# A chunked state-space stage: decay prefixes from one scan per batch, x weighted on ScalarE, scores made four chunks at a time

## The reference

```python
zxbca = x @ W_in.T
x_t, z_t, b_t, c_t, a_log = split(zxbca)      # 32 heads, 64 wide
decay = exp(-exp(a_log))                       # one number per token and head
def step(states, inp):
    xt, bt, ct, dec = inp
    states = states * dec[:, :, None, None] + xt[..., None] * bt[:, :, None, :]
    yt = einsum('bhpn,bhn->bhp', states, ct) + xt * D
    return states, yt
y = scan(step, ...); y = y * silu(z_t); y = layernorm(y) * gamma + beta
return y @ W_out.T
```

## Time and profile before

| | us |
|---|---|
| median of 3 runs (lowest, highest) | 2042.74 (2037.55, 2045.25) |
| the profiled execution | 2042.33 |
| its span | 2040.3 |
| busy: PE / PEld / DVE / ACT / POOL | 1826.9 / 1623.2 / 1412.7 / 781.5 / 734.3 |
| mean granted TensorE clock | 0.965 of 2.4 GHz |
| chain that ended last, by engine | PE 63%, DVE 15%, POOL 8%, issue 8%, ACT 6% |

### The profile page before, as it was taken

How to read it: one execution, slowest core, us unless ns; L and a number is a source line. 1 busy time by engine, 2 the same in 40 slices (tenths; PEclk the granted TensorE clock), 3 DMA queues, 4 the chain that set the end, 5 groups by cost and what they waited for, 6 DMA issues and landing times.

```text
span 2040.3 us, 33554 instructions
## 1 busy us (share of the span) xinstructions
PE 1826.9 (90%) x11376; PEld 1623.2 (80%) x11376; DVE 1412.7 (69%) x3170; ACT 781.5 (38%) x1846; POOL 734.3 (36%) x772
## 2 busy tenths in 40 slices
PE   5998999999898888988969989999998988888889
PEld 4996777888787777877849967778887877788878
DVE  5555887545688888887455558875456888888874
ACT  3334454332333333334632344543323333333355
POOL 1012443001566666662010124430014666666610
PEclk9999999999999999998969999999998999999989
DMA  2120000021112211210021200000211122121100
GB/s 77 45 100 16 16 17 23 11 73 47 49 58 66 66 60 59 66 55 1 16 70 45 100 16 17 16 23 10 73 45 48 61 65 65 66 65 60 50 6 16
DMA packets 39446, 93.75 MB, mean 46 GB/s; under 512 B 3632, under 2 KB 12464, under 8 KB 38768
## 3 DMA queue, kind: packets, MB, share of 16 engines
q1 hardware_dynamic: 39280, 91.62, 13.4%
HBM read 89.24 MB, written 2.36 MB: 45 GB/s over the span
## 4 chain that ended last, share of the span: by engine, by line
PE 63%; DVE 15%; POOL 8%; issue 8%; ACT 6%; DMA 0%; DVEq 0%; SPq 0%; POOLq 0%; ACTq 0%
PE ps L495 27%; PE ps L567 11%; PE ps L536 5%; DVE pdec L1513 4%; PE ps L789 3%; PE ps L559 3%; POOL w_in_lo L477 3%; PE ps L781 2%; POOL y L472 2%; PE ps L771 2%; PE ps L523 2%; PE ps L669 2%; ACT cTz L1119 2%; POOL rb L420 2%; PE ps L650 2%
## 5 line engine op out<-in xcount | busy, mean ns | idle before, releaser
L472 POOL TENSOR_TENSOR y<-yg,sz 128x128 f32<-128x128 f32 x256 | 220.4, 861 | 324.7 <-DVE yg L1561 324.7
L1131 ACT ACTIVATE xz_x<-ps 128x128 f32<-128x128 f32 x256 | 71.2, 278 | 426.3 <-PE ps L495 366.2
L567 PE MATMUL ps<-w_out,yT 128*128 128x256 f32 x1024 | 226.0, 379 | 0.0
L567 PEld LDWEIGHTS ps<-w_out,yT 128*128 128x128 f32 x1024 | 192.3, 190 | 24.9
L420 POOL TENSOR_TENSOR rb<-ra,rb 128x512 f32<-128x512 f32 x80 | 118.6, 1483 | 221.8 <-DVE rb L1372 221.7
L468 POOL TENSOR_TENSOR xd<-xz_x,d_row 128x128 f32<-128x128 f32 x256 | 176.6, 690 | 47.2 <-ACT sz L1134 47.2
L781 PEld LDWEIGHTS ps<-xw,b_tok 128*128 128x128 f32 x448 | 79.9, 189 | 115.4 <-issue 106.6
L781 PE MATMUL ps<-xw,b_tok 128*128 128x128 f32 x448 | 91.0, 285 | 83.5 <-DVE ssm_state L1549 46.9
L1513 DVE TENSOR_TENSOR_SCAN pdec<-dec,dstart 64x512 f32<-64x512 f32 x128 | 161.6, 1263 | 0.9
L789 PE MATMUL ps<-xz_x,mt 128*128 128x128 f32 x1024 | 160.3, 280 | 1.6 <-DVE yg L1561 1.6
L1529 DVE TENSOR_TENSOR xw<-ps,lmat 128x128 f32<-128x128 f32 x256 | 72.9, 285 | 124.6 <-ACT sz L1134 124.6
(11 more groups left out here) (172 smaller groups left out, 4993.6 us busy)
## 6 DMA issues: line engine op xcount, KB each, us to landing
dec<-dec_dram SPq DMA_DIRECT2D x64, 512.0 KB, 3.9
w_raw<-in_w_in SPq DMA_DIRECT2D x32, 512.0 KB, 3.6
w_raw<-in_gu SPq DMA_DIRECT2D x14, 704.0 KB, 4.1
w_raw<-in_w_qkv SPq DMA_DIRECT2D x8, 768.0 KB, 4.5
dn_raw<-in_dn SPq DMA_DIRECT2D x14, 384.0 KB, 4.7
w_out<-in_w_o SPq DMA_DIRECT2D x2, 2048.0 KB, 11.3
w_out<-in_w_out SPq DMA_DIRECT2D x2, 2048.0 KB, 8.5
x_res<-in_x SPq DMA_DIRECT2D x8, 256.0 KB, 3.6
```

Source lines behind the costliest of these rows:

```text
L472: nc.gpsimd.tensor_tensor(y[:, c, bass.ds((2 * i + w) * P, P)], yg[:, s], sz[:, s], ALU.mult).then_inc(s_out.sem, 1)
L567: mm = nc.tensor.matmul(ps[:, 4 + s, 0:DM], yT[:, s, t, :], w_out[:, t, :], start=(t == 0), stop=(t == NT - 1))
```

## The change

- **Decay prefixes.** `pdec` is no longer scanned per unit. Once per batch, in the last FFN group, DVE scans all 32 heads at a time (`decay_prefix`: 32 partitions x 1024 tokens, in five steps), SP writes the decays (with chunk starts zeroed) and the prefixes to DRAM, and loads the prefixes per unit as two broadcasts of 64 partitions into `pdec`. `dstart`, its copies and the memset in `dec` are gone.
- **Weighted x.** `xw` is made by ACT, two copies of 128 x 64 from PSUM with the column of `lmat` as per-partition scale, between `xz_x` and `sz`.
- **Scores.** `unit_scores` makes the four score matmuls of a unit in one run, in the third chunk of the unit before, and DVE weights them two chunks at a time (two products of 512 columns). The matmul itself, one of 256 columns for both heads against the zero-padded `cTz`, is the same as before.
- **Order.** `b_turn` moves to the head of the fourth chunk, ACT's `c_copy` and `btok_copy` move ahead of `xz_copy`. The increments of `settled` go. The first weight load of the stage comes behind the writes of the prefixes, and the two `lmat` scans of the first unit move from chunks 3 and 4 of the last FFN group to 5 and 6.

```diff
@@ sync @@
-                sp.wait_ge(s_dec.sem, s_dec.done(b))
-                sp.dma_start(dec_dram, dec_t[:]).then_inc(dec_out, 16)
-                sp.wait_ge(dec_out, 16 * (b + 1))
...
-                        weights(split_ssm(b, h), a["w_in"][bass.ds(h, 1)].rearrange("g p c -> p (g c)"), KT * XZBC)
...
-                            sp.wait_ge(s_scan.sem, s_scan.done(2 * n + hf - 2))
-                            sp.dma_start(dec[:, :, toks], dec_dram[bass.ds(2 * h, 2), toks].partition_broadcast(P)).then_inc(dec_in[hf], 16)
+                sp.wait_ge(s_prep, 5 * (b + 1))
+                sp.dma_start(dec_dram[0], dec_t[:]).then_inc(dec_out, 16)
+                sp.dma_start(dec_dram[1], dec_p[:]).then_inc(dec_out, 16)
+                sp.wait_ge(dec_out, 32 * (b + 1))
+                for h in range(HP):
+                    n = b * HP + h
+                    weights(split_ssm(b, h), a["w_in"][h], KT * XZBC)
+                    sp.wait_ge(s_out.sem, s_out.done((n - 2) * NC + NC - 1))
+                    sp.dma_start(d_row[:, h % 2, :], a["d_skip"][h:h + 1, :].broadcast_to([P, P])).then_inc(d_in[h % 2], 16)
+                    for hf in range(2):
+                        u = 2 * n + hf
+                        toks = slice(hf * HALF, (hf + 1) * HALF)
+                        sp.wait_ge(s_scan.sem, s_scan.done(2 * (u - 2) + 1))
+                        sp.dma_start(dec[:, :, toks], dec_dram[0, 2 * h:2 * h + 2, toks].partition_broadcast(P)).then_inc(dec_in[hf], 16)
+                        sp.wait_ge(s_st.sem, s_st.done(4 * (u - 2) + 3))
+                        for k in range(2):
+                            sp.dma_start(pdec[64 * k:64 * k + 64, toks],
+                                         dec_dram[1, 2 * h + k:2 * h + k + 1, toks].broadcast_to([64, HALF])).then_inc(pdec_in[hf], 16)
@@ tensor @@
+                    for j in range(4):
+                        c, m = 4 * hf + j, 4 * u + j
+                        if ahead and j == 3:
+                            b_turn(u + 1, nhf)
+                        if ahead or j < 3:
+                            project_xz(m + 1, nw if j == 3 else n % 2, (c + 1) % NC)
+                        if ahead and j == 2:
+                            unit_scores(u + 1, nhf)
+                        ssm_update(u, m, c)
+                        ssm_outputs(u, m, c)
+                        if ahead and j == 0:
+                            if hf == 1:
+                                ssm_weights(n + 1)
+                            project_b(u + 1, nw, nhf)
+                        if ahead and j == 1:
+                            project_c(u + 1, nw, nhf)
@@ scalar @@
                 def first_pair():
-                    act.wait_ge(dec_out, 16 * (b + 1))
+                    act.wait_ge(dec_out, 32 * (b + 1))
                     ssm_prep(0, 0)
...
-                                         ps[:, 2 + s, 0:P].rearrange("p (h c) -> p h c", c=64), ACT.Copy)
+                                         ps[:, 2 + s, 0:P].rearrange("p (h c) -> p h c", c=64), ACT.Copy).then_inc(s_xcopy.sem, 1)
+                    for h in range(2):
+                        if c % 4 == 0:
+                            act.wait_ge(s_scan.sem, s_scan.done(2 * u + h))
+                        ins = nc.scalar.activation(xw[:, s, 64 * h:64 * h + 64], ps[:, 2 + s, 64 * h:64 * h + 64], ACT.Copy,
+                                                   scale=lmat[:, h, (c + 1) * P - 1:(c + 1) * P])
+                    ins.then_inc(s_xw.sem, 1)
                     act.wait_ge(s_out.sem, s_out.free(m, 2))
...
+                        if ahead and j == 2:
+                            c_copy(u + 1, 1 - hf)
+                        if ahead and j == 3:
+                            btok_copy(u + 1, 1 - hf)
+                        if ahead or j < 3:
+                            xz_copy(u + (j == 3), m + 1, (c + 1) % NC)
+                        if ahead and j == 1:
+                            b_copy(u + 1, 1 - hf)
+                        if hf == 0 and j == 0 and n + 1 < HP:
+                            ssm_prep(n + 1, (n + 1) % 2)
@@ vector @@
+                    nc.vector.memset(dec_s[:], 0.0).then_inc(s_prep, 1)
...
+                    for hf in range(2):
+                        toks = slice(hf * HALF, (hf + 1) * HALF)
+                        nc.vector.tensor_tensor_scan(dec_p[:, toks], dec_t[:, toks], dec_s[:, toks], 0.0, ALU.mult, ALU.add).then_inc(s_prep, 1)
...
+                        ssm_next_state(m, c)
+                        add_skip(m, c)
...
+                        if j < 2:
+                            decay_scan(u + 1, j)
+                        if j == 2:
+                            c_decayed(u + 1)
+                            decayed_scores(u + 1, 0)
+                        if j == 3:
+                            decayed_scores(u + 1, 1)
+                u0 = 2 * b * HP
+                ffn_group(b, G0 + 1, 1, False, {0: decay_prefix, 5: lambda: decay_scan(u0, 0), 6: lambda: decay_scan(u0, 1)}, last=True)
```

More of the change, by code:

```diff
@@ L784, in ssm_outputs @@
                     out = ps[:, 6, 0:P]
-                    pe.wait_ge(s_mt.sem, s_mt.done(m))
                     pe.wait_ge(s_xcopy.sem, s_xcopy.done(m))
                     pe.wait_ge(s_yg.sem, s_yg.done(m - 1))
+                    if c % 2 == 0:
+                        pe.wait_ge(s_mt.sem, s_mt.done(2 * u + c % 4 // 2))
                     for h in range(2):
-                        nc.tensor.matmul(out, mt1[:, c % 2, h * P:(h + 1) * P], xz_x[:, c % 2, h * P:(h + 1) * P],
+                        nc.tensor.matmul(out, mt1[:, u % 2, c % 4, h, :], xz_x[:, c % 2, h * P:(h + 1) * P],
@@ new lines, in ssm_unit @@
+                def ssm_unit(u):
+                    hf = u % 2
+                    n, ahead = u // 2 - b * HP, u < 2 * HP * (b + 1) - 1
+                    nw, nhf = (n + hf) % 2, 1 - hf
+                    for j in range(4):
+                        c, m = 4 * hf + j, 4 * u + j
[13 more added lines that the diff above has]
+                            project_c(u + 1, nw, nhf)
@@ new lines, in xz_copy, with ssm_unit @@
+                    ins.then_inc(s_xw.sem, 1)
+                    act.wait_ge(s_out.sem, s_out.free(m, 2))
+                    nc.scalar.activation(sz[:, s, :], ps[:, 2 + s, P:2 * P], ACT.Silu).then_inc(s_sz.sem, 1)
+                def ssm_unit(u):
+                    hf = u % 2
+                    n, ahead = u // 2 - b * HP, u < 2 * HP * (b + 1) - 1
+                    for j in range(4):
+                        c, m = 4 * hf + j, 4 * u + j
+                        if ahead and j == 2:
[8 more added lines that the diff above has]
+                            ssm_prep(n + 1, (n + 1) % 2)
@@ L1154, in _ @@
                 c_copy(u, 0)
[L1155 removed]
+                xz_copy(u, u * 4, 0)
                 btok_copy(u, 0)
                 gate_silu(b, GRP - 1)
[L1158 to L1160 removed]
+                for u in range(2 * b * HP, 2 * (b + 1) * HP):
+                    ssm_unit(u)
                 end_phase(act, b, 5)
@@ new lines, in decay_scan @@
+                def decay_scan(u, h):
+                    hf = u % 2
+                    toks = slice(hf * HALF, (hf + 1) * HALF)
+                    if h == 0:
+                        dve.wait_ge(dec_in[hf], 16 * (u // 2 + 1))
+                        dve.wait_ge(s_mt.sem, s_mt.done(2 * (u - 2) + 1))
+                        dve.wait_ge(s_xw.sem, s_xw.done(4 * u - 5))
+                    nc.vector.tensor_tensor_scan(lmat[:, h, toks], dec[:, h, toks], ident4[:, 0:HALF], 0.0, ALU.mult, ALU.add).then_inc(s_scan.sem, 1)
@@ L1601, in _, with ssm_unit @@
-                for i in range(0, HP // 2 - 1):
-                    ssm_pairs(i, False)
-                ssm_pairs(HP // 2 - 1, True)
+                def ssm_unit(u):
+                    hf = u % 2
+                    n, ahead = u // 2 - b * HP, u < 2 * HP * (b + 1) - 1
+                    for j in range(4):
+                        c, m = 4 * hf + j, 4 * u + j
+                        ssm_next_state(m, c)
+                        add_skip(m, c)
+                        if n == HP - 1 and c < 2 * EARLY:
+                            dve.wait_ge(s_out.sem, s_out.done((b * HP + 4 * EARLY) * NC - 1))
+                            dve.wait_ge(o_yn.sem, o_yn.done(4 * (b * 2 + 1) * NC - 1))
+                            inner_stats(c // EARLY, c // EARLY, c % EARLY)
+                        if not ahead:
+                            continue
+                        if j < 2:
[5 more added lines that the diff above has]
+                            decayed_scores(u + 1, 1)
```

231 lines of the change are left out of this document (56 added, 175 removed).

## The result

The changed kernel takes **2057.54 us** (median of 4 runs, 2054.37 to 2064.2), the kernel before, run beside it, 2040.35 (2037.55 to 2045.25): ratio **1.0086**, interval 1.0052 to 1.0120. So it is slower by 0.9%, a small step but clear of the interval; the forecast was 2016, range 1985 to 2050, with 0.16 for slower. The profiled execution took 2064.2, its span is 2062.4 and its mean granted clock 0.955 (before 0.965).

A forecast was written before the change was run, and what follows sets the result against it. The prediction took the SSM stages as bound by PE plus one DVE burst per unit. From 2042.3 us it took 35 for 32 pairs at 25.05 instead of 26.17, added 10 for the stage starts: 2017, put at 2016; range 1985 to 2050.

The forecast's parts named there:

- new wait 2: Next pair's w_raw load, queued behind pdec loads on SP, lands late and delays ACT and the scores: 0.65 us a pair.
- the weights land late: Rival, 12%: w_raw lands slower beside other loads; from a landing of 4.4 no gain is left, at 4.7 2051 us.
- the clock falls after each stop: Rival, 7%: the new waits, 2 us together, cause a low-clock stretch in every pair: +38 us, 2054.
- The waits before the increment: PE's waits for DVE's state before line 781, 1.37 and 1.48 us a pair, claimed to go.
- POOL's piece: Last quarter of the weights' low part, awaited by PE before project_b of chunk 4: 0.2 us a pair (0.51 before).
- PE's bare work: PE's work in a pair without its lost time, taken as 22.8 us.
- Wait 1: Scores one project_xz behind project_c wait for ACT's copies of c: 0.7 us a unit, 1.4 a pair.
- the start of the stage: In the last FFN group, prefix writes delay the first w_raw, so ACT and PE stand: +5 us a batch, +10 in all.
- the 6.2: Upper bound for the prefix write to DRAM at the stage's start, 6.2 us against 3 taken: +6 us in all.
- The weights are no wait: Rival, 16%: ACT reaches the split late anyway, or the load lands in under 3 us: 1992 us.
- The lost time only moves: Rival, 10%: POOL's late pieces cost 0.9 us more per pair at chunk 4: +29, about 2043 us, no change.
- DVE's burst: The two pdec scans, 2.54 us per unit on DVE, held to delay the state PE wants; claimed to go.

The follow-up runs named there:

- experiment 2: Changed kernel, next pair's weight load ahead of the two pdec loads but still behind SP's wait for the state; 1990.65 us, ratio 0.9721.
- experiment 6: Kernel before, with SP made to wait for the last chunk's state before loading the next pair's weights; 2064.57 us, ratio 1.0074.
- experiment 1: Changed kernel, next pair's weight load issued ahead of SP's wait for the state and the pdec loads; 1983.68 us, ratio 0.9686.
- experiment 3: Kernel of experiment 1, with the next unit's scores moved behind update and outputs of the third chunk; 1929.02 us, ratio 0.9417.
- experiment 8: Kernel of experiment 3 with the stage's first weights loaded early, unsplit by write waits, plus POOL's four weight pieces behind chunks 0, 1, 2, 2; 1901.58 us, ratio 0.9275.
- experiment 10: Kernel of experiment 3 with the stage's first weights early, plus two unused 64 x 512 scans per unit put back on DVE; 1952.87 us, ratio 0.9522.
- experiment 7: Kernel of experiment 3 with the stage's first weights early, and xw moved back from ACT to DVE; 1929.31 us, ratio 0.9419.
- experiment 11: Changed kernel, next pair's weight load moved further back on SP, behind d_row and the first half's dec; 2172.69 us, ratio 1.0604.

## Why the prediction was wrong

**The step that failed is new wait 2.** "Two `pdec` issues at some 0.4 each; `w_raw` at 0.85; it lands 3.6 later, at 4.45." It was issued at 1.28 and used 4.4 later in the middle, at 5.6 (in the pair shown 4.86 later, at 6.14). Both parts come from the `pdec` loads beside it in the queue. They take 1.09 together to issue, and the load behind them 0.58 in place of 0.35. And it lands 0.8 slower with their 256 KB under way, whether they stand ahead of it or right behind it (4.4 in the changed kernel and in experiment 2, 3.6 in experiment 6, where there are none). I took the median of the earlier trace rows, loads with nothing near them in the queue. The sentence "the `pdec` loads are out before, by issue order", which I held against the rival "the weights land late", was no argument: by these numbers the `pdec` loads cost the landing the same just before as just after. That rival had nothing left of the gain from a landing of 4.4, and 4.4 it was. ACT's part behind that was well sized (3.34 from the start of the high part to the end of the copies; 3.72 by the sum), and so was PE's request at 6.8. So the wait of the first unit came out at 2.73 in the pair shown instead of 1.35, and wait 2 at 1.62 a pair (26.27 - 24.65, experiment 1) instead of 0.65: 31 us. Experiment 2 put the weights where the forecast had them, at 4.5, and got about the forecast's pair, 25.17 against 25.05, partly by luck: wait 2 was smaller there and what experiment 3 gained larger than forecast.

**The second step is the clock.** The sum took 32 undisturbed pairs of 26.17 against 32 of 25.05 and so left the low stretches as they were, 26.80 - 26.17 = 0.63 a pair. They became 27.56 - 26.27 = 1.29: 21 us more. The granted clock says the same: (1 - clock) x length, summed over the 30 pairs, rises from 20 to 42 us. In all PE stood no longer than before, 26.27 - 22.93 = 3.3 us in an undisturbed pair against 3.4, but one stop was longer, 1.8 to 4.1 where nearly all had been 1.2 or 1.3. The row at 0.51 lies right behind a wait of 2.5 before the scores. The rival "the clock falls after each stop" had the mechanism and came near in time (2054), but from waits of 2 us in all; with the waits as small as forecast it doesn't happen (experiment 2), and it needed the rival "the weights land late" with it. I had given the two 12% and 7% as if apart; the second follows from the first. The rule of the Trainium skill in "TensorE: Matmul & The Clock Gate", Part 1, that lack of activity lowers the clock, agrees with these runs (21 of 30 pairs under 1.00 here, 2 in experiment 1); what I made of it, that the waits would be shorter than before, was my own wrong size.

**Point by point.** The waits before the increment went, as forecast. PE's work with POOL's piece is 22.93 a pair (23.0 forecast; experiment 3); but 22.8 as PE's bare work was too much, since experiment 8 makes a pair in 22.56. Wait 1, with all that moving the scores brought, is 1.72 a pair (1.4; experiments 1 and 3). An `xw` pair takes 0.51 (0.48). Four deviations of 0.97, 0.66, 0.32 and -0.07 make 1.88 a pair, 60 us. Against this stand the start of the stage and its end. The stage of batch 0 began 3.4 us later than before (515.09 for 511.71), and that of batch 1 0.8 later, net of what lies ahead (forecast 5 each): 6 us better. The stages together grew by 17.7 where 32 x 0.76 = 24 would follow from the pairs: 6 less in the first and last pairs, where I had put 1. 60 - 6 - 5 = 49; the span is 2062.4 where the forecast's is 2014, 48 more.

At the start the stops were sized well (ACT until 499.7, forecast 501.2; PE 4.1, forecast 4.6), and the write was cheap, 2.0 and 2.2 for the two. The Trainium skill, "DMA: Bandwidth & Descriptors", in the section on the anatomy of one DMA (not on bandwidth, as I wrote), has completion to HBM as the slow case. That the 6.2 would be the rule by it, and the sum 6 us higher, was my reading and not the page's; these two writes do not bear it out.

**The other rivals.** "The weights are no wait" is what experiment 1 made. "The lost time only moves" to POOL is out: its wait at chunk 4 is worth 0.37 a pair with everything else gone (experiment 8).

**Where the gain went.** Removing DVE's burst was right (experiment 10: 35 us even in the new order), `xw` on ACT too (experiment 7: 14), and with two lines of SP's and PE's order put right the same change is worth 5.8% (experiment 3). It was spent on one chain: SP's queue, the load, ACT's high part, the copies of c, the scores. Either link cut frees most of it: the scores alone bring 6.0%, the weights alone 4.0%, both 6.7%.

## What to carry to other kernels

When a load is moved behind others in one queue, price it by its new neighbours on both sides: the issue times of those ahead, its own longer issue, and the bytes under way beside it; a median of loads that stood alone is the lower bound. Then put the consumer of the chain's last link as far behind the producer as its order allows: here 0.9 us of other matmuls before the scores were worth more than the early load. And where a forecast lengthens a stop on PE, the clock's price is part of that rival, not one beside it; compare means over all pairs, not undisturbed ones.

## What the runs showed of the hardware that I had not expected

- A 512 KB load took 3.6 from issue to use with no `pdec` load near it (experiment 6), 4.4 right behind two loads of 128 KB (the changed kernel), 4.4 right ahead of them (experiment 2) and 6.3 behind a load of 512 KB (experiment 11), each the middle of some 28, all from one queue. Single loads of a kernel spread from 4.1 to 6.4, so one pair of the timeline does not price them.
- On SP's queue the issue of the load right behind the pair of `pdec` issues took 0.58 instead of 0.35, and the pair 1.09.
- With a stop of 1.8 to 4.1 us on PE once a pair (and one of 0.6), 21 of 30 pairs had a stretch at the clock's lower level, 1.2 GHz (granted 0.51 in the one shown); in the kernel before, with two stops of mostly 1.2 and 1.3, it was 10 of 30, in experiment 1, with stops of 0.6 twice a pair, 2 of 30, and in experiment 11, with stops of 3.9 to 7.0 once a pair, 25 of 27. What in the stop decides it, and why 9 pairs escape, stays open: no run varied the stop by itself, and pairs with stops of 1.8, of 2.2 and of 2.5 fell on both sides.
- A scaled copy of 128 x 64 from PSUM on ACT with one per-partition operand took 0.31 (the two of a chunk 0.51 together).
